# A decoder layer on one core: attention head outputs turned in 32x32 blocks by VectorE, and the order of work into the expert stage

## The reference

```
out = softmax(q k^T / 4) v            # 16 heads of 16, 2048 queries, 1601 keys
x = x + out @ Wo + bo
xn = rmsnorm(layernorm(x)) * gamma    # tokens
sn = rmsnorm(slot_embeds) * slot_gamma    # 8 experts x 128 slots
logits = xn @ sn^T                    # 2048 x 1024
dispatch = softmax(logits over tokens);  combine = softmax(logits over slots)
slots = dispatch^T @ xn;  h = gelu(slots @ w1 + b1);  eo = h @ w2 + b2
x = x + combine @ eo
```

## Time and profile before

| | us |
|---|---|
| median of three runs (1382.36 to 1387.23) | 1383.48 |
| the profiled execution | 1383.01 |
| its span, first to last instruction | 1381.1 |
| TensorE busy | 1274.8 (92%) |
| ScalarE busy | 936.4 (68%) |
| VectorE busy | 740.7 (54%) |
| GpSimd busy | 384.2 (28%) |

### The profile page before, as it was taken

How to read it: one execution, slowest core, us unless ns; L and a number is a source line. 1 busy time by engine, 2 the same in 40 slices (tenths; PEclk the granted TensorE clock), 3 DMA queues, 4 the chain that set the end, 5 groups by cost and what they waited for, 6 DMA issues and landing times.

```text
span 1381.1 us, 14607 instructions
## 1 busy us (share of the span) xinstructions
PE 1274.8 (92%) x5512; PEld 619.4 (45%) x5512; DVE 740.7 (54%) x824; ACT 936.4 (68%) x1218; POOL 384.2 (28%) x280
## 2 busy tenths in 40 slices
PE   8679987989789987999799999999999999899999
PEld 4234543435343543466322232222222245588988
DVE  5999999999999999863620010010000147650011
ACT  5857855685667655833599999999999966752300
POOL 2646765666566757631100000000000100000000
PEclk9789987999999997999899999999999999999999
DMA  6435675243224334478340000000000000203601
GB/s 197 162 114 149 211 219 178 101 146 126 92 92 155 129 120 130 152 226 192 88 128 1 0 1 1 0 1 1 0 1 1 1 0 31 92 0 131 265 16 46
DMA packets 43014, 127.72 MB, mean 92 GB/s; under 512 B 6103, under 2 KB 21400, under 8 KB 39545
## 3 DMA queue, kind: packets, MB, share of 16 engines
q1 hardware_dynamic: 42942, 126.75, 28.4%
HBM read 109.64 MB, written 17.09 MB: 92 GB/s over the span
## 4 chain that ended last, share of the span: by engine, by line
PE 64%; DVE 21%; ACT 8%; issue 6%; DMA 0%; DVEq 0%; POOL 0%; SPq 0%; ACTq 0%
PE ps L2148 15%; PE ps L2135 14%; DVE ps L1264 11%; PE ps L1927 5%; PE ps L2295 4%; PE ps L2338 4%; PE ps L2219 4%; DVE arena L1275 3%; PE ps L1988 3%; PE ps L1973 3%; PE ps L1707 2%; ACT ps L851 2%; PE ps L2313 2%; PE ps L2326 2%; PE ps L2163 1%
## 5 line engine op out<-in xcount | busy, mean ns | idle before, releaser
L1096 ACT ACTIVATE arena<-ps,bound 128x1536 f32<-128x1536 f32 (+1 forms) x278 | 409.8, 1536 | 29.4 <-PE ps L2135 29.2
L657 POOL TENSOR_TENSOR arena<-arena 128x1024 f32<-128x1024 f32 x127 | 298.3, 2350 | 216.7 <-DVE arena L1275 183.4
L1264 DVE TENSOR_TENSOR_SCAN ps<-ps,arena 128x1024 f32<-128x1024 f32 x128 | 300.6, 2349 | 11.4 <-ACT ps L851 10.1
L1927 PE MATMUL ps<-arena,ident 128*128 128x512 f32 x512 | 236.5, 608 | 3.9 <-DVE arena L1275 3.9
L2135 PE MATMUL ps<-arena 97*128 97x512 bf16 (+1 forms) x832 | 229.0, 387 | 5.9 <-issue 5.4
L2148 PE MATMUL ps<-arena 128*32 128x512 f32 (+1 forms) x1664 | 222.2, 606 | 1.0 <-ACT arena L1096 0.3
L851 ACT ACTIVATE ps<-arena 128x512 f32<-128x512 f32 x256 | 166.2, 682 | 51.5 <-DVE arena L1275 47.1
L640 POOL TENSOR_TENSOR rstd<-ve,mhalf 128x4 f32<-128x4 f32 (+3 forms) x23 | 25.3, 1102 | 539.8 <-DVE ve L1567 465.4
L2135 PEld LDWEIGHTS ps<-arena 97*128 97x128 bf16 (+1 forms) x832 | 63.8, 100 | 229.6 <-ACT arena L1096 147.8
L1275 DVE TENSOR_TENSOR arena<-ps,arena 128x1024 f32<-128x1024 f32 x128 | 156.0, 1218 | 8.2 <-DMA arena<-bc_scratch 1.2
L1594 DVE COPY arena<-ps 128x512 f32<-128x512 f32 x16 | 11.1, 692 | 272.6 <-PE ps L2148 272.6
(11 more groups left out here) (204 smaller groups left out, 1362.4 us busy)
## 6 DMA issues: line engine op xcount, KB each, us to landing
arena<-bc_scratch SPq DMA_DIRECT2D x128, 512.0 KB, 4.4
arena<-in_mw SPq DMA_DIRECT2D x16, 1024.0 KB, 10.0
qx_scratch<-arena SPq DMA_DIRECT2D x48, 128.0 KB, 3.3
arena<-qx_scratch SPq DMA_DIRECT2D x4, 1536.0 KB
arena<-kx_scratch SPq DMA_DIRECT2D x1, 4803.0 KB
kx_scratch<-arena SPq DMA_DIRECT2D x36, 128.0 KB, 3.8
arena<-vx_scratch SPq DMA_DIRECT2D x1, 3328.0 KB
vx_scratch<-arena SPq DMA_DIRECT2D x6, 512.0 KB, 4.6
```

Source lines behind the costliest of these rows:

```text
L657: product = pool.tensor_tensor(dbu[:, w % DR], du[:, DP * p:DP * p + DP], over(bg[:, w // BG % 2, n % BG], DP), ALU.mult)
L1096: act.activation(flat(prob[k % PSLOTS])[0:n, 0:w], banks(SPAN * (k % 2), SPAN)[0:n, 0:w], ACT.Exp, bias=bound[0:n, 3:4], scale=HD ** -0.5) ...
L1264: dve.tensor_tensor_scan(decay_banks(w), decay_banks(w), flat(dbu[:, w % DR]), carry[:, DP * p, n:n + 1], ALU.mult, ALU.add).then_inc(S["s ...
L1927: last = mm(bank(x), ident[:, :], state(2 * j + s)[:, x], start=False, stop=(j % HP == HP - 1 and (j in SUMMED or s == 1)))
```

## The change

- `heads_out` no longer copies. VectorE's 32x32 block transpose takes bank 6 to SBUF (a head's 32 rows become 32 columns, for 32 tokens on 32 partitions). It takes the reciprocal of the sums, multiplies, and, after each second group, transposes the pair of groups back in blocks into `att`. The rows of `Wo` are permuted on the host to fit. The first `attend` of the next group waits for the first of these four operations.
- `turn_heads`, `turn_attended`, `heads_normed` and `heads_turned` are gone. Each of the first three chunks has eight pieces, in the steps 74 to 102, 142 to 170 and 210 to 238 (every fourth). The last chunk has two tail pieces, in tiles 0 and 1.
- The slot embeddings are turned in the idle steps 22, 26, 30 and 34 of the attention, through bank 7, and VectorE copies them.
- The first four token tiles are normed by VectorE in steps 245 to 248, and the first is turned and copied in step 250. In the loop VectorE norms tile `t+4`.
- One `turn_combine` stands in each of the tiles 3 to 15 (13 in the loop, before 12). The last chunk's statistics are in tiles 2 to 5 (before 7 to 9).
- Column maxima: both halves are turned together right after the running maximum. VectorE's order is the last row maximum, reduce half 0, its four diagonals, reduce half 1, two subtractions of half 0, the other four diagonals, then the remaining subtractions.

```diff
-MICRO = CT + DK + DK * CT
+MICRO = DK * CT
...
             def heads_out(q):
-                if q >= NG and q % NG == 0:
-                    dve.wait_ge(S["oq_ps"], q // NG * CT)
+                c, k, a = q // NG, q % NG // 2, q % 2
+                if q >= 2:
+                    dve.wait_ge(S["at_ready"], q - 1)
                 dve.wait_ge(S["pv_done"], KB * (q + 1))
-                dve.tensor_copy(ot[:, q % NG], bank(6)).then_inc(S["o_evac"], 1)
+                dve.transpose(flat(ot[:, a]), bank(6)).then_inc(S["o_evac"], 1)
+                dve.wait_ge(S["o_evac"], q + 1)
+                dve.reciprocal(orec[:, a].unsqueeze(2), ot[:, a, :, HD:HD + 1]).then_inc(S["orec_ready"], 1)
+                if c:
+                    dve.wait_ge(S["att_ready"], (c - 1) * DK + k + 1)
+                dve.wait_ge(S["orec_ready"], q + 1)
+                dve.tensor_tensor(nrm[:, k, :, a * HD:a * HD + HD], ot[:, a, :, 0:HD],
+                                  orec[:, a].unsqueeze(2).to_broadcast([P, TB, HD]), ALU.mult).then_inc(S["at_ready"], 1)
+                if a:
+                    if c:
+                        dve.wait_ge(S["o_ps"], 2 * c)
+                    dve.wait_ge(S["at_ready"], q + 1)
+                    dve.transpose(att[:, k], flat(nrm[:, k])).then_inc(S["att_ready"], 1)
...
             def out_piece(c, s):
-                if s < CT:
+                if c == "slots":
                     if s == 0:
-                        pe.wait_ge(S["o_evac"], c * NG + NG)
+                        pe.wait_ge(S["sn_ready"], NE)
+                    else:
+                        pe.wait_ge(S["snt_ready"], s)
+                    for x in range(4):
+                        last = turn(bank(7)[:, tok(x)], se[:, 4 * (s % 2) + x, tok(s // 2)])
+                    last.then_inc(S["snt_ps"], 1)
+                elif c == "tokens":
+                    pe.wait_ge(S["x2_ready"], 2 * (NC - 1))
+                    turn_tokens(0)
+                else:
+                    i, k = s // DK, s % DK
+                    if s == 0:
+                        pe.wait_ge(S["att_ready"], c * DK + DK)
...
+                if j == scaled_step + 1:
+                    dve.memset(xn[:, :, DM:DM + 1], 1.0).then_inc(S["xn_one"], 1)
+                    normed_tokens(0, 1)
+                if scaled_step + 1 < j <= scaled_step + NORMED:
+                    normed_tokens(j - scaled_step - 1, j - scaled_step)
...
-            pe.wait_ge(S["sn_ready"], NE)
-            for n in range(4):
-                for x in range(4):
-                    last = turn(bank(n)[:, tok(x)], se[:, 4 * (n % 2) + x, tok(n // 2)])
-                last.then_inc(S["snt_ps"], 1)
...
             for t in range(TT):
                 if t + 1 < TT:
                     turn_tokens(t + 1)
                 logits(t, 0)
-                for e in combined(t)[:-1]:
-                    turn_combine(e)
                 logits(t, 1)
-                if t < TAIL:
+                if t < 2:
                     tail_piece(t)
-                for e in combined(t)[-1:]:
-                    turn_combine(e)
+                if t >= LAG:
+                    turn_combine(t - LAG)
...
+            column_max(0)
+            column_diagonals(0)
+            column_max(1)
+            for t in range(2):
+                shifted(0, t)
+            column_diagonals(1)
+            for t in range(2, TT):
+                shifted(0, t)
+            for t in range(TT):
+                shifted(1, t)
```

More of the change, by code:

```diff
@@ L289, in decoder_layer @@
         se = Stack(prob_at + G * C).take(NE, DM)
-        snt = Stack(prob_at).take(DK, MS)
         e1 = Stack()
@@ L296, in decoder_layer @@
         region = e1.at
-        xnt = e1.take(2, DK, P)
+        xnt = Stack(wq_at).take(2, DK, P)
         mrun = e1.take(MS)
@@ L433, in attends, with heads_step @@
             return range(attended[j - 1] if j else 0, attended[j])
+        def heads_step(q):
+            return next(k for k in range(len(attended)) if KB * q + KB - 1 in attends(k))
+        idle_steps = [k for k in range(len(attended)) if not attends(k)]
         for c in range(NC - 1):
-            done = attended.index(NV * (c + 1))
-            places = [k for k in range(done + 1, len(attended)) if not attends(k)]
-            assert attended[places[CT - 1]] < NV * (c + 1) + KB
+            places = [k for k in idle_steps if k > heads_step(c * NG + NG - 1)][:MICRO]
+            assert places[-1] < heads_step((c + 1) * NG + 1)
             for s in range(MICRO):
                 piece_at[places[s]] = c, s
-        assert attended[-1] == NC * NV and len(piece_at) == MICRO * (NC - 1)
+        last_piece = places[-1]
+        assert attended[-1] == NC * NV
+        for n in range(4):
+            piece_at[[k for k in idle_steps if k > heads_step(0)][n]] = "slots", n
+        scaled_step = max(last_piece + 4, heads_step(NC * NG - 3))
+        token_step = next(k for k in idle_steps if k > scaled_step + 4)
+        piece_at[token_step] = "tokens", 0
         block = ctx.enter_context(nc.Block())
@@ L1131, in _ @@
                     turned_tokens(t + 1)
-                for e in combined(t)[:-1]:
-                    turned(e)
                 act.wait_ge(S["l_ps"], t + 1)
                 act.activation(lg[:, t], banks(2 * (t % 2), 2), ACT.Copy).then_inc(S["l_copy"], 1)
-                for e in combined(t)[-1:]:
[L1137 to L1146, removed]
+                if t >= LAG:
+                    turned(t - LAG)
+            turned(INSIDE)
+            combine_weights(TT - 1)
+            turned(INSIDE + 1)
+            for t in range(2):
+                shifted_exp(0, t)
+            turned(INSIDE + 2)
+            for t in range(2, TT):
+                shifted_exp(0, t)
+            for t in range(TT):
+                shifted_exp(1, t)
             for x in range(NE):
@@ L1664, in _, with column_max, column_diagonals @@
                 last_run(t)
+            token_max(TT - 1)
             dve.wait_ge(S["xn_one"], 1)
-            for n in range(2):
+            def column_max(n):
                 dve.wait_ge(S["mt_ps"], n + 1)
                 dve.tensor_reduce(mcol[:, 4 * n:4 * n + 4], bank(n).rearrange("p (e n) -> p e n", n=P), AX, ALU.max).then_inc(S["mcol_ready"], 1)
+            def column_diagonals(n):
                 dve.wait_ge(S["mcol_ready"], n + 1)
@@ L1671, in _, with shifted @@
                     dve.tensor_scalar(mdiag[:, x], ident[:, :], mcol[:, x:x + 1], None, ALU.mult).then_inc(S["mdiag_ready"], 1)
-                if n == 0:
-                    token_max(TT - 1)
-            for n in range(2):
+            def shifted(n, t):
+                half_row = lg[:, t, 512 * n:512 * n + 512]
                 dve.wait_ge(S["mb_ps"], n + 1)
[L1676 to L1679, removed]
+                dve.wait_ge(S["l_exp"], t + 1)
+                dve.tensor_tensor(half_row, half_row, bank(2 + n), ALU.subtract).then_inc(S["l_sub"], 1)
+            column_max(0)
+            column_diagonals(0)
+            column_max(1)
+            for t in range(2):
+                shifted(0, t)
+            column_diagonals(1)
+            for t in range(2, TT):
+                shifted(0, t)
+            for t in range(TT):
+                shifted(1, t)
             for x in range(NE):
@@ L2150, in attend @@
                 last.then_inc(S["pv_done"], 1)
[L2152 to L2160, removed]
             def attention_out(c, i, k, n):
@@ L2188, in out_piece, with turn_tokens @@
                     attention_out(c, i, k, 7)
+            def turn_tokens(t):
+                pe.wait_ge(S["xn_ready"], t + 1)
+                if t == 1:
+                    pe.wait_ge(S["xnt_ready"], 1)
+                if t == 2:
+                    pe.wait_ge(S["o_evac"], NC * NG)
+                if t >= 3:
+                    pe.wait_ge(S["xnt_ready"], t - 1)
+                for k in range(DK):
+                    last = turn(ps[:, 6 + t % 2 if t else 7, tok(k)], xn[:, t, tok(k)])
+                last.then_inc(S["xnt_ps"], 1)
             for j in range(len(attended)):
@@ L2218, in logits @@
                 for k in range(DK):
-                    last = mm(bank(2 * (t % 2) + n), xnt[:, t % 2, k], snt[:, k, n * 512:n * 512 + 512],
+                    last = mm(bank(2 * (t % 2) + n), xnt[:, t % 2, k], snt[DK * k + n],
                               start=(k == 0), stop=(k == DK - 1))
@@ L2222, in logits, with tail_piece @@
                     last.then_inc(S["l_ps"], 1)
[L2224 to L2233 removed]
+            def tail_piece(b):
+                if b == 0:
                     pe.wait_ge(S["att_ready"], NC * DK)
[L2235 to L2237 removed]
+                for i in (2 * b, 2 * b + 1):
+                    for k in range(DK):
+                        attention_out(NC - 1, i, k, 4 + b)
             def turn_combine(t):
@@ L2257, in _, with turn_maxima, spread_maxima @@
                 logits(t, 0)
-                for e in combined(t)[:-1]:
```

(29 more changed lines are left out.)

122 lines of the change are left out of this document (38 added, 84 removed).

## The result

The changed kernel takes 1375.97 us (median of four runs, 1373.96 to 1376.29). The kernel before took 1385.36 in the four runs beside them (1382.36 to 1387.45). The ratio is 0.9936, 95% interval 0.9922 to 0.9950: 9.4 us less by the medians, faster by a little over 0.5%. The forecast was 1373.0, 10.3 us less than before. Beside the first experiments one execution of the kernel before took 7115 us, where all others took 1382 to 1388; the ratios leave it out.

A forecast was written before the change was run, and what follows sets the result against it. TensorE was taken as the bound. Pieces -4.1, head groups' wait +1.8 and the experts part -8.0 make -10.3: profiled 1383.01 to 1372.7, median 0.47 above, stated as 1373.0 us; range 1369.5 to 1380.0.

The forecast's parts named there:

- into the experts: From the last `attend` to the slot matmuls: earlier start, shorter loop and column maxima, together -8.0 us.
- The new wait of the head groups: Attention group ends and step 210: TensorE waits for VectorE's transposes instead of the copy, +1.8 us.
- The price B: Time of VectorE's block transpose in `heads_out`, which no profile row showed: taken as 0.72 us.
- The rival of the slow transpose: Bank 6 at group ends: the block transpose is slow; about 1379.9 us at 1.22 each; chance 0.12.
- The prediction's other estimate: VectorE's block transpose priced from two sections of the Trainium skill: 0.71 us, making the term +1.7.
- The pieces: Attention's idle steps: 14 fewer transpose pieces at 0.30 us, plus 0.1 for one token piece: -4.1 us.
- the rival without a gain in the attention: Attention: ScalarE's queue sets the step, so fewer pieces gain nothing; 1377.3 us; chance 0.09.
- Start: Last `attend` to first logits: only two transposes of tile 1 remain there, -2.96 us.
- loop: Expert tile loop: six pieces go (-2.64), stalls shrink (-0.90), one combine comes in (+0.87).
- maxima: Last logits to slot matmuls: reordered column maxima take 9.37 us instead of 11.73, -2.36.
- The wait at tile 3: Expert loop: TensorE waits 0.66 us for ScalarE's copy, behind an exponential waiting for VectorE's late row maximum.
- bound the early tiles: Rival, tiles 0 to 5: VectorE's work repeats a 0.7 us stall per tile; 1376 us; chance 0.11.

The follow-up runs named there:

- the first experiments: Follow-up runs of the changed kernel with edits; the first listed moves the third chunk's output pieces one idle step later: 1373.52 us.
- the second trace of before: The kernel before, profiled once more with no edit: 1384.26 us.
- the last experiments: Closing follow-up runs; the last listed is the changed kernel with third-chunk pieces one idle step later and all diagonals ahead of the subtractions: 1370.51 us.

## Why the prediction came out as it did

The direction and the main mechanism were right, and the time lies in the range, 3 us above the forecast. The profiled execution parts these: it took 1376.05 where 1372.7 was foreseen for it, 3.35 more. Of that 1.9 are from one step, 210, and 1.4 came up ahead of the changed code, in parts that differ from one execution to the next; what is left are differences of 0.3 and less that nearly cancel. (The prediction's own sum, 1372.7 and 0.47, makes 1373.2 and not 1373.0.) Against the second trace of before, in which the attention starts as slowly as after:

| | forecast | measured |
|---|---|---|
| attention | -2.3 | 437.62 - 438.08 = -0.5 |
| into the experts | -8.0 | 82.40 - 90.32 = -7.9 |

Of the 0.5, steps 4 to 8 alone are 0.35, where the change does nothing. What the change did to the attention is -3.8 for the pieces and +3.7 for the head groups: nothing.

**The new wait of the head groups** is the step that was mis-sized. Its length was right: 1.62 us foreseen, 1.79 measured, with the same four operations behind it, 0.03 to 0.11 apart instead of 0.03 to 0.06. What was missing is what TensorE does after such a gap: 1.6 to 1.7 us more at the lower clock. So step 210 cost 9.68 - 6.28 = 3.40 us and not 1.49. The forecast had kept full clock throughout, as the rows of before showed it. The term of the prediction was 0.33 + 1.49 = 1.8; it is 0.3 + 3.4 = 3.7. The 0.3 is ten ends at 0.717 - 0.692 each, one end less than the prediction counted.

**The price B.** 0.72 was taken, 0.717 and 0.711 were measured. TensorE waits 0.15 us at a group end, where the prediction had 0.13 for the copy, and with the transpose doubled ten ends followed the formula. The rival of the slow transpose falls with it. The prediction's other estimate, 0.71, is as near.

**The pieces.** Six pieces less in each of three chunks gave 1.74, 1.65 and 1.67 us, and four slot pieces cost 1.29: -3.8 with one token piece in it, forecast -4.1. The rest is spread over these stretches, which hold group ends too; I did not part it further. ScalarE did not set the steps, so the rival without a gain in the attention falls.

**Into the experts.** Start -2.80 (forecast -2.96), loop -2.81 (-2.64 - 0.90 + 0.87 = -2.67), maxima -2.31 (-2.36). The wait at tile 3 is there with 0.36 us of idle TensorE instead of 0.66, at the place and for the cause that were named. VectorE does not bound the early tiles. That the maxima's gain would have been 1.6 larger in a plainer order was not seen in the prediction, though its own working had the two subtractions on the path.

**The median.** The traces give -0.5 - 7.9 = -8.4 us, the medians -9.4. Executions of one kernel lie up to 5 us apart, in the Mamba part and in the first steps above all, and I cannot tell which share of the last microsecond is the change's. The seven executions of the kernel before that were taken beside the last experiments have a median of 1384.23, and from that one the difference is 8.3.

## What to carry to other kernels

Price a piece of work in a full queue by the step with it against the step without it, and look for the first place where its producer has less time than everywhere else: here two of three chunks were covered and one was not. Where TensorE then stands for long, look at the granted clock behind the gap as well as at the gap. Here 1.79 us were followed by the lower clock in each of three traces, and 1.72 and 1.73 us, in another place, by none; where it falls, it can cost as much again. Either move the consumer or give TensorE other work. When a queue is reordered to feed one consumer early, check that nothing queued ahead of that consumer waits for what was put back. Where a price is multiplied by a number of places, take that number from the schedule: one of the eleven group ends here was none.

## What the runs showed of the hardware

- A gap of 1.79 us in TensorE's work, after hundreds of microseconds at full clock, was followed by some 3 us at 1.2 GHz; filled with 1.75 us of transposes, it was not. The ten gaps of 0.8 to 0.9 us at group ends left the clock at 1.00, and one of 2.5 us was again followed by 0.50.
- VectorE's 32x32 block transpose of 128x512 float32 takes 0.717 us from PSUM and 0.711 from SBUF, 3% more than the plain copy (0.692).
- The first four steps of the attention take 6.91 or 7.84 us with the same program, by when the granted clock rises.
